# A mixture-of-experts layer and a GRU scan on one core: 64-token chunks, kept weights, gate banks that hold the inputs

## The reference

```python
# layer 0: four gated experts and a shared one; weights w_be per batch from a small gate
for e in range(E):
    h = gelu(x @ ew1[e] + eb1[e])                 # 256 -> 1024
    out += w_be[:, e] * mask[e] * (h @ ew2[e] + eb2[e])   # 1024 -> 256
x = x + out + gelu(x @ sw1 + sb1) @ sw2 + sb2
# layer 1: a GRU over the 1024 tokens, one after the other
z = sigmoid(x_t @ W_z + h @ U_z + vz)
r = sigmoid(x_t @ W_r + h @ U_r + vr)
hh = tanh(x_t @ W + (r * h) @ U + vh)
h = (1 - z) * h + z * hh
out_t = x_t + h
```

## Time and profile before

| | |
|---|---|
| median of 3 runs | 2235.7 us (2235.5 to 2245.23) |
| span of the profiled execution (the page gives no other time of it) | 2236.9 us |
| first scan of step 0 (L730) | 124.72 us |
| instructions | 108229 |
| PE busy, by the profile | 95% |
| mean granted TensorE clock | 0.982 |

### The profile page before, as it was taken

How to read it: one execution, slowest core, us unless ns; L and a number is a source line. 1 busy time by engine, 2 the same in 40 slices (tenths; PEclk the granted TensorE clock), 3 DMA queues, 4 the chain that set the end, 5 groups by cost and what they waited for, 6 DMA issues and landing times.

```text
span 2236.9 us, 108229 instructions
## 1 busy us (share of the span) xinstructions
PE 2118.5 (95%) x43019; PEld 1776.9 (79%) x43019; DVE 1200.3 (54%) x10473; ACT 686.9 (31%) x3670; POOL 344.0 (15%) x684
## 2 busy tenths in 40 slices
PE   7999999999999999999999999999999999989998
PEld 6788888888888888888888888888888888765665
DVE  5245555555555555555555555555554555555555
ACT  2333333333333332333333333333333333222222
POOL 3011111111111111111112111111111111110000
PEclk8999999999999999999999999999999999899999
DMA  5411111111111111111111111111111111000000
GB/s 160 133 53 48 44 47 39 44 45 43 49 39 42 49 44 41 44 42 44 47 41 42 46 46 42 41 46 42 44 46 39 42 49 44 12 4 4 4 4 4
DMA packets 143478, 97.21 MB, mean 43 GB/s; under 512 B 13664, under 2 KB 142999, under 8 KB 143004
## 3 DMA queue, kind: packets, MB, share of 16 engines
q1 hardware_dynamic: 141840, 90.49, 14.2%
q10 hardware_dynamic: 1164, 0.07, 0.0%
HBM read 88.41 MB, written 2.10 MB: 40 GB/s over the span
## 4 chain that ended last, share of the span: by engine, by line
PE 88%; DVE 5%; ACT 4%; issue 3%; POOL 0%; POOLq 0%; ACTq 0%; DVEq 0%
PE c_ps L917 21%; PE r_ps L917 20%; PE y_ps L874 16%; PE up_ps L856 13%; PE z_ps L917 12%; DVE h_parts L730 3%; PE up_ps L945 3%; ACT c_ps L507 3%; PE xp_ps L888 2%; DVE p_parts L716 1%; ACT r_ps L507 1%; PE xp_ps L898 1%; PE y_ps L829 0%; DVE hidden L278 0%; PE z_ps L903 0%
## 5 line engine op out<-in xcount | busy, mean ns | idle before, releaser
L917 PE MATMUL r_ps<-h_parts,u_high 128*128 128x20 f16 x8192 | 558.9, 180 | 81.7 <-DVE h_parts L730 49.5
L917 PEld LDWEIGHTS r_ps<-h_parts,u_high 128*128 128x128 f16 x8192 | 424.6, 96 | 261.4 <-DVE h_parts L730 149.3
L917 PE MATMUL z_ps<-h_parts,u_high 128*128 128x20 f16 x8192 | 565.6, 179 | 0.0
L917 PE MATMUL c_ps<-p_parts,u_high 128*128 128x40 f16 x8192 | 526.7, 182 | 14.9 <-DVE p_parts L716 1.9
L856 PE MATMUL up_ps<-feat,up_w 128*128 128x128 f32 (+1 forms) x2380 | 526.6, 314 | 0.0
L917 PEld LDWEIGHTS c_ps<-p_parts,u_high 128*128 128x128 f16 x8192 | 412.8, 96 | 138.4 <-issue 41.0
L874 PE MATMUL y_ps<-hidden,down_w 128*128 128x128 f32 (+1 forms) x2380 | 498.0, 314 | 5.6 <-DVE hidden L278 5.6
L716 DVE SCALAR_TENSOR_TENSOR p_parts<-r_ps,h_hist 128x4 f16<-128x4 f32 x1024 | 166.5, 163 | 528.9 <-ACT r_ps L507 528.3
L917 PE MATMUL z_ps<-h_parts,u_mid 128*128 128x20 f16 x4096 | 438.0, 179 | 0.0
L917 PEld LDWEIGHTS z_ps<-h_parts,u_high 128*128 128x128 f16 x8192 | 424.8, 96 | 0.0
L507 ACT ACTIVATE r_ps<-r_ps 128x4 f32<-128x4 f32 x1024 | 161.8, 158 | 744.5 <-PE r_ps L917 744.4
(11 more groups left out here) (132 smaller groups left out, 2157.9 us busy)
## 6 DMA issues: line engine op xcount, KB each, us to landing
up_w<-in_L_cond_ew SPq DMA_DIRECT2D x256, 128.0 KB, 2.4
down_w<-in_L_cond_ew SPq DMA_DIRECT2D x256, 128.0 KB, 2.1
up_w<-in_L_cond_sw SPq DMA_DIRECT2D x64, 128.0 KB, 2.4
down_w<-in_L_cond_sw SPq DMA_DIRECT2D x64, 128.0 KB, 2.1
x_rows<-in_x SPq DMA_DIRECT2D x8, 256.0 KB, 4.9
out<-out_rows SPq DMA_DIRECT2D x128, 16.0 KB, 1.8
cf<-in_L_cond_C_r SPq DMA_DIRECT2D x1, 256.0 KB, 5.8
cf<-in_L_cond_C_z SPq DMA_DIRECT2D x1, 256.0 KB, 6.0
```

What stands on the lines that cost most here:

```text
L917: return mm(gate_ps[g][:, m * SC + t * B:m * SC + t * B + width], w[:, g, k, m * P:(m + 1) * P], moving, start=False, stop=i == LO and k = ...
```

## The change

- **Chunks** are 64 tokens. The inputs of a chunk are projected straight into the gate banks: each gate bank holds two regions of 256 columns, one for the chunk in work and one for the next. DVE first copies the bias into the region (`seed`, 6 copies of 128 columns a chunk), PE adds the projection on top (`project`). `xpart`, `split` and `inject` are gone.
- **Weights** of all branches stay in SBUF (10 loads of 1 MB in place of 640). Hidden tiles are 128 by 128, twelve are held, and POOL scales each with the expert's weight (or zero where masked). `gate_scale` is gone.
- **Windows**: a table `SIDE` for the 64 steps of a chunk. Window 0 takes one unit, window 1 two, from step 0 on, until the 162 units of a chunk's layer 0 are out (step 55); the residual add follows, and the 12 projections, now of 128 columns, stand at steps 57 to 60. Steps 61 to 63 have none. A unit's wait stands at the unit.
- **The state**: two scans instead of three; the word lies in SBUF (`h_cur`, `p_cur`), the tanh results in banks of their own. DVE adds the output of each step (L623 after) in place of POOL's work. On PE gate z starts after the low part of r. The two factors of the state both read a full tensor `half_s`.
- **Waits**: DVE counts high part, word and low part in one semaphore, `part_ready`; the wait for it is written before the wait for ACT.
- **Prologue**: layer 0 of the first 64 tokens alone, four branches (expert 2 is masked there), 32 tiles, and no tile beyond it.

The core of the diff, shortened. The table of the windows:

```diff
+    for t in range(1, CT, STEPS):
+        SIDE[t, 1].append((TURN, 0, 0))
...
+        if i < BR * HT:
+            units += [(UP, i, 0), (UP, i, 1)]
+        if i == LAG:
+            units += [(BIAS, 0, 0), (BIAS, 0, 1)]
+        if i >= LAG:
+            units += [(DOWN, i - LAG, 0), (DOWN, i - LAG, 1)]
+    for t in range(CT):
+        for w in range(2):
+            while units and len(SIDE[t, w]) < 1 + w:
+                SIDE[t, w].append(units.pop(0))
...
+            if kind == UP and k == 1:
+                GELU_STEP.setdefault(t + w, []).append(i)
```

DVE, one step, first r*h and then the state:

```diff
-                    dve.wait_ge(act_done, gate0 + 1)
-                    dve.wait_ge(state, s0 - 1)
-                    dve.scalar_tensor_tensor(p(HI), tr, 1.0, prev, ALU.add, ALU.mult).then_inc(part_ready, 1)
-                    dve.scalar_tensor_tensor(sq(product), tr, 1.0, prev, ALU.add, ALU.mult).then_inc(state, 1)
-                    dve.wait_ge(state, s0 + 1)
-                    dve.tensor_tensor(p(LO), sq(product), p(HI), ALU.subtract).then_inc(part_ready, 1)
+                dve.wait_ge(part_ready, parts + H_WORD)
+                dve.wait_ge(act_done, s * GATES + R + 1)
+                for to in (p_top[:, :, 0:B], p_cur[:, :, :]):
+                    dve.scalar_tensor_tensor(to, sq(tanh_r), 1.0, sq(h_now), ALU.add, ALU.mult
+                                             ).then_inc(part_ready, 1)
+                dve.wait_ge(part_ready, parts + PARTS_STEP + P_WORD)
+                dve.tensor_tensor(p_low[:, :, 0:B], p_cur[:, :, :], p_top[:, :, 0:B], ALU.subtract
+                                  ).then_inc(part_ready, 1)
...
-                    dve.wait_ge(act_done, gate0 + 3)
-                    dve.wait_ge(state, s0 + 3)
...
+                dve.wait_ge(blended, (s + 1) * BLEND_STEP + 2)
+                dve.wait_ge(act_done, s * GATES + C + 1)
+                for to in (h_top[:, 0, :], h_cur[:, :]):
+                    dve.tensor_tensor_scan(to, cand, blend[:, :], 0.0, ALU.mult, ALU.add
+                                           ).then_inc(part_ready, 1)
+                dve.wait_ge(part_ready, parts + PARTS_STEP + H_WORD)
+                dve.tensor_tensor(h_low[:, 0, :], h_now, h_high, ALU.subtract).then_inc(part_ready, 1)
+                dve.tensor_scalar(half_h[:, :], h_now, -0.5, None, ALU.mult).then_inc(blended, 1)
...
+                last = dve.scalar_tensor_tensor(
+                    out_feat[:, body % 2, :, row * B:(row + 1) * B], sq(h_now), h_unscale[:, :],
+                    feat[:, :, s * B:(s + 1) * B], ALU.mult, ALU.add)
```

PE, the projection, the waits of the windows, and those of an up unit:

```diff
-                    for kind, e, unit in FFN_UNITS.get((t + window, 1 - window), ()):
-                        if unit == 0:
-                            (up_ready if kind == UP else down_ready)(*ffn, e)
...
+            def up(c, i, k):
...
+                    if n >= 2:
+                        pe.wait_ge(gelu_done, n - 1)
...
+            def project(c, g, m, k):
+                at = (c % 2) * REGION + m * COLS
+                mm(gate_ps[g][:, at:at + COLS], wx[:, g, k, m * P:(m + 1) * P], feat[:, k, c * COLS:(c + 1) * COLS],
+                   start=False, stop=False, skip_group_check=True)
```

More of the change, by code:

```diff
@@ L68, in moe_gru_kernel @@
     b_in = [b_r, b_z, b_h]
[L72 to L82, removed]
@@ L83, in moe_gru_kernel @@
-    assert not units
[L85 to L93, removed]
@@ new lines, in moe_gru_kernel @@
+    TILES = [[(e, j) for e in (FIRST_BRANCHES if c == 0 else range(BR)) for j in range(HT)] for c in range(CH)]
+    TILE0 = [sum(map(len, TILES[:c])) for c in range(CH + 1)]
+    SCALED = {}
+    for c in range(CH):
+        n_scaled = 0 if c < 2 else SCALED[TILE0[c] - 1]
+        for i, (e, j) in enumerate(TILES[c]):
+            n_scaled += e < E
+            SCALED[TILE0[c] + i] = n_scaled
+    UP, DOWN, BIAS, TURN, PROJECT = "up", "down", "bias", "turn", "project"
+    SIDE = {(t, w): [] for t in range(CT) for w in range(2)}
@@ new lines, in moe_gru_kernel @@
+    for t in range(1, CT, STEPS):
+        SIDE[t, 1].append((TURN, 0, 0))
+    units = []
+    for i in range(BR * HT + LAG):
+        if i < BR * HT:
[8 more added lines that the diff above has]
+                SIDE[t, w].append(units.pop(0))
+                DOWN_STEP = t
@@ new lines, in moe_gru_kernel @@
+    assert not units
+    GELU_STEP = {}
+    for (t, w), some in SIDE.items():
+        for kind, i, k in some:
+            if kind == UP and k == 1:
+                GELU_STEP.setdefault(t + w, []).append(i)
+    RESIDUAL_STEP = DOWN_STEP + 1
+    projections = {w: [(g, m, k) for g in ((C,), (R, Z))[w] for m in range(KC) for k in range(KC)] for w in range(2)}
+    for t in range(RESIDUAL_STEP + 1, CT):
+        for w in range(2):
+            while projections[w] and len(SIDE[t, w]) < 1 + w:
+                SIDE[t, w].append((PROJECT, *projections[w].pop(0)))
@@ L333, in _, with load_mats, load_up @@
-            with sp.Fori(CH * BODIES - lag, CH * BODIES) as n:
-                store_body(n)
-            sp.wait_ge(out_written, (CH * BODIES + 1) * 2 * 16)
+            def load_mats(to, some, done):
+                for g in range(GATES):
+                    sp.dma_start(to[:, g, :, :], some[g].rearrange("(k p) n -> p k n", p=P)).then_inc(done, 16)
+            def load_up(e):
+                w1 = ew1[e, :, :] if e < E else sw1
+                sp.dma_start(up_w[:, e, :, :], w1.rearrange("(k p) n -> p k n", p=P)).then_inc(up_in[e], 16)
@@ new lines, in _ @@
+            load_down(first[-1])
+            load_mats(wx, w_in, wx_in)
+            for e in range(BR):
+                if e not in first:
+                    load_up(e)
+                    load_down(e)
+            for n in range(CH * BODIES):
+                sp.wait_ge(turned_copied, n + 1)
+                for b in range(B):
+                    sp.dma_start(out[b, n * STEPS:(n + 1) * STEPS, :], out_rows[b:SC:B, n % 2, :]
+                                 ).then_inc(out_written[n % 2], 16)
@@ L338, in _ @@
+            for i in range(2):
+                sp.wait_ge(out_written[i], CH * BODIES // 2 * B * 16)
         @block.gpsimd
@@ new lines, in _, with residual, side @@
+            dve.memset(cand, 0.0)
+            make_rows(CT, T).then_inc(rows_made, 1)
+            scale_first(24, len(TILES[0]))
+            def residual(c, k):
+                if k == 0:
+                    dve.wait_ge(down_done, TILE0[c + 1])
+                here = feat[:, k, c * COLS:(c + 1) * COLS]
+                dve.tensor_tensor(here, y_ps[:, k * COLS:(k + 1) * COLS], here, ALU.add).then_inc(feat_ready, 1)
+            for k in range(KC):
+                residual(0, k)
+            def side(c, t, window):
+                if c == CH - 1:
+                    return
+                if (t, window) in SEEDS:
+                    seed(c + 1, *SEEDS[t, window])
+                if t == RESIDUAL_STEP:
+                    residual(c + 1, window)
@@ L871, in down @@
[L871 to L892 removed]
+                return last
```

914 lines of the change are left out of this document (375 added, 539 removed).

## The result

The changed kernel takes 2412.0 us (median; 2409.7 to 2414.2), where the kernel before takes 2236.9 in the same comparison: 1.077 of its time, 95% interval 1.075 to 1.080. The forecast was 2288 us with a range of 2215 to 2350. The sign was right, the size was not: the loss is 175 us and not 51.

A forecast was written before the change was run, and what follows sets the result against it. The prediction took a chain of latencies, 2.00 us a step, as the bound. It summed first scan 57 + 1023 x 2.16 (2210) + gelu 4 + clock 12 + end 6 = 2289, median 1 us below: 2288 us, range 2215 to 2350.

The forecast's parts named there:

- What bounds the kernel: Recurrence step: a chain of latencies sets the pace, not busy PE; 2.00 us a step, 1023 x 2.00 = 2046 us.
- The swapped waits: DVE's waits for ACT: a late separate wait costs 0.09 us, twice a step, 0.18 us; bounds 0.06 and 0.13.
- rival 1: DVE's swapped waits cost only the lower bound, 0.06 us each; 2227 us; chance 0.15.
- Rival 2: DVE's swapped waits cost nothing, next instruction being already decoded; step 1.98 us, 2110 us; chance 0.11.
- The word in SBUF, one scan less: DVE's state scans: word moved to SBUF and third scan removed save 20 ns a step, from 10 to 30.
- Side work: Work beside the recurrence: POOL's scaling of a tile hides; one late step a chunk for a gelu, 4 us.
- The clock: Chunk borders: clock falls in empty steps 61 to 63, two slow steps a chunk; 12 us, from 0 to 40.
- rival 4: Chunk starts: clock stays low for six slow steps instead of two, 23 us more, 2311 us; chance 0.12.
- Prologue: Work ahead of the first scan: first scan at 57 us, from 52 to 72; gain 68 us.
- Fit of the side work: PE windows: with the 0.6 us gap behind gate c 0.09 longer, two units of 0.26 to 0.30 us fit.
- rival 3: DVE's swapped waits cost more, 0.13 us each; given as 2377 us; chance 0.10.

The follow-up runs named there:

- own_act: The changed kernel with act_done again the instruction's own wait in all three places of a step where DVE waits for ACT; 2164.5 us.
- before_sep: The kernel before, with only the waits ahead of r*h and the scan of h reordered so that act_done is the separate wait; 2425.3 us.
- word_psum: The changed kernel with the word of h in PSUM and tanh r in SBUF; 2337.4 us.
- pool_late: The changed kernel with POOL starting a tile's scaling only after the low part of h of the gelu's step; 2312.0 us.
- own_c: The changed kernel with the order of the waits turned back ahead of the scan of h alone; 2249.6 us.
- late_fill_gelu: The changed kernel with POOL's late start, fill matmuls in empty window slots and earlier gelus, act_done still the separate wait; 2262.4 us.
- own_fill_gelu: own_act plus fill matmuls in window slots without side work, and gelus issued in the step of a tile's last unit; 2097.4 us.

## Why the prediction was wrong

- *What bounds the kernel*: right. The chain of latencies sets the step: turning back one wait or both moved the undisturbed step by 0.07 us each.
- *The swapped waits*: right as the term that decides the sign, somewhat large: 0.07 us a wait and not 0.09, near the 0.06 of rival 1. PE's weight load (0.06) was the best guide; PE's matmul and ACT's pair (0.09), and above all DVE's memset pair, said too much. Rival 2 (costs nothing) fell with own_act and before_sep.
- *The word in SBUF, one scan less*: 20 ns a step forecast, in 10 to 30; 30 to 33 ns measured (2.107 against before_sep's 2.137, own_act's 1.967 against 2.000). Some 10 ns of it is the word of h, by word_psum; no run parts the rest. These two items made the forecast's step 0.053 us too long, 54 us in all, which hid part of what follows.
- *Side work, "POOL's scaling of a tile is due three tiles later and hides"*: this step failed, for 100 us by pool_late (111 in the table above). I asked when its result is needed and not what it holds while it runs. Before, the low part read the word from PSUM and was never stretched; the change brought the word to SBUF, and the swapped wait put the low part just behind the start of a scaling of 0.40 us. own_c, word_psum and pool_late each remove the term in a different way. The forecast had the word's move only as a matter of 7 ns.
- *The clock*: the mechanism was named, empty windows and slow units behind them, but sized at 2 steps and 0.4 us each. The border with its gelus costs 5.1 us a chunk, 77 us and not 16. The forecast also had the lower clock cost the bare recurrence nothing; in the kernel before, four steps at 0.50 from 1940.9 us on take 2.067 us each against 2.000. The earlier trace rows had 0.50 for a whole stretch; rival 4, with six slow steps, was nearest (12 + 23 us of clock), and too small still, for the end of the chunk suffers as well: steps 57 and 58 take 2.67 and 2.65 us by the medians.
- *Prologue*: 67.5 for 57 us; 6.6 of it is PE's wait for POOL's chain, and layer 0 itself ended 4 us late. The same idle time of 7.2 us ahead of its first scaling stands in the earlier trace rows, and I left it out; and I let the split of U begin when U lands and end at 41, so that the scalings of W had nothing to queue behind.
- *Fit of the side work*: right. Window work hides in the undisturbed step.
- *Two sums*: 57 + 1023 x 2.24 + 22, rival 3, is 2371 us and not 2377; and rival 1 with the shorter prologue is 2222, so the 2215 of the range's lower end has 7 us that no term gives. Neither moves the forecast.

Without POOL's term and with the border as forecast the time would have been about 2412 - 111 - 61 = 2240 us, no change. So the sign came out right only with the help of what I had missed: the waits, 143 us, were about paid for by the prologue (57), the shorter pieces (34) and the long steps of before that went (60). That sum is worked out and no run stands for it; late_fill_gelu comes near it, with 2262 us.

## What to carry to other kernels

Write the wait that is met last as the instruction's own, and look at this for each instruction on a chain. When a tensor moves from PSUM to SBUF, list which POOL work can run beside its readers on DVE, and who starts first: 0.07 us somewhere else can turn 0 into 0.23 us. Fill windows that a plan leaves empty, and when you price a low clock, count the steps behind the gap too: here it stayed low for 16 us after the units were back.

## What the runs showed of the hardware

- A separate wait that is met last costs 0.07 us over the instruction's own, in DVE's two places of both kernels (0.26 against 0.19 us).
- DVE and POOL, both on SBUF: with POOL 0.03 us ahead, DVE's instruction of 0.16 us takes 0.39; with DVE 0.05 us ahead it takes 0.16 and its successor 0.39. POOL's own instruction is 0.40 us in each case.
- With each step 0.14 us longer by the waits the clock is low more often: before_sep spent 303 us at 1.2 GHz, the kernel before 81; late_fill_gelu 127 us, own_fill_gelu 30. Why is not shown.
- Open: what fills the 7.3 us before POOL's first scaling of U; it stands in all thirteen kernels, with 7.1 to 8.1 us, and no run here takes it away.
